# Queries and keys produced in natural layout, one graph at a time, with the values' product directly behind them

## The reference, cut to what matters

```python
x = x + gnn(layernorm(x), adj)          # 12 heads of 32
#   q, k, v = x@Wq.T, x@Wk.T, x@Wv.T + bv
#   a = softmax(q k^T * 384**-0.5 + adj) ; o = a v ; o@Wo.T + bo
x = x + ffn(layernorm(x))
#   top 2 of 4 experts by the graph's mean; h = act_e(u@w1_e.T + b1_e); y = sum gate * (h@w2_e + b2_e)
#   layernorm(y + u) * ln_g + ln_b      # u is the ffn's normalised input; act: gelu, silu, mish, gelu
```

## Time and profile before

| | before |
|---|---|
| three runs, us | 1636.82, 1639.47, 1640.29 (median 1639.47) |
| profiled execution, us | 1638.12 |
| its span, first to last instruction, us | 1636.0 |
| mean granted clock of the matrix engine | 0.993 of 2.4 GHz |
| stage 1, scores of step 3 to scores of step 63, us | 52.19 to 699.37 |
| length of a full step of stage 1, us | 10.70 |
| busy share of PE, DVE, ACT, POOL over the span | 97%, 74%, 58%, 42% |

### The profile page before, as it was taken

The page is one execution under the profiler, slowest core; times in us unless marked ns, Lnnn a source line. Parts: engine busy times, 40 slices in busy tenths (PEclk is TensorE's granted clock), DMA queues, the critical chain, the costliest instruction groups (busy, mean ns, idle before and its releaser), DMA issues.

```text
span 1636.0 us, 46011 instructions
## 1 busy us (share of the span) xinstructions
PE 1590.5 (97%) x12720; PEld 1528.0 (93%) x12721; DVE 1209.8 (74%) x3750; ACT 955.6 (58%) x2819; POOL 689.6 (42%) x1106
## 2 busy tenths in 40 slices
PE   8999999999999999779999999999999999999998
PEld 7999999999999999769999999999999999999998
DVE  5788888888888888657766666676776767677766
ACT  6899999999999988753422232333334323243332
POOL 3787888878888777531111111111111111111112
PEclk9999999999999999889999999999999999999999
DMA  6444433455545543673222222222222222222211
GB/s 190 153 138 138 136 129 132 147 168 182 176 169 172 182 134 133 253 301 105 71 74 74 74 74 74 74 74 74 67 70 71 65 74 74 74 74 65 83 59 45
DMA packets 93804, 189.09 MB, mean 116 GB/s; under 512 B 10337, under 2 KB 57441, under 8 KB 92385
## 3 DMA queue, kind: packets, MB, share of 16 engines
q1 hardware_dynamic: 91664, 170.17, 31.6%
q10 hardware_dynamic: 1872, 15.73, 2.5%
HBM read 108.80 MB, written 77.07 MB: 114 GB/s over the span
## 4 chain that ended last, share of the span: by engine, by line
PE 89%; DVE 3%; issue 2%; ACT 2%; DMA 1%; POOL 1%; DVEq 1%; ACTq 0%; POOLq 0%; SPq 0%
PE bank L460 69%; PE bank L534 5%; PE bank L667 5%; PE bank L487 3%; PE bank L557 3%; PE bank L574 2%; PE bank L543 1%; PE bank L566 1%; DMA ut_scratch<-ut_out 1%; DVE half_t L1371 1%; DVE inverse L1378 1%; DVE inverse L1374 1%; ACT at_hi L944 0%; ACT inverse L951 0%; ACT prob L737 0%
## 5 line engine op out<-in xcount | busy, mean ns | idle before, releaser
L460 PE MATMUL bank<-w_hi,ut_in 128*128 x1536 | 423.7, 343 | 0.8 <-issue 0.4
L460 PE MATMUL bank<-w_both,at_hi 128*128 x1524 | 389.1, 336 | 7.4 <-DVE at_lo L1343 7.3
L737 ACT ACTIVATE prob<-att,heads 128x128 f32<-128x128 f32 x768 | 297.4, 390 | 14.2 <-DVE heads L1108 10.3
L460 PEld LDWEIGHTS bank<-w_both,at_hi 128*128 128x128 f32 x1524 | 274.3, 188 | 12.3 <-issue 12.2
L460 PEld LDWEIGHTS bank<-w_hi,ut_in 128*128 128x128 f32 x1536 | 281.5, 189 | 1.3 <-issue 1.3
L460 PE MATMUL bank<-w_lo,ut_in 128*128 x768 | 258.2, 336 | 0.0
L460 PE MATMUL bank<-w_both,at_lo 128*128 x762 | 255.3, 335 | 0.0
L875 ACT ACTIVATE hid<-hid 128x384 f32<-128x384 f32 x192 | 95.1, 526 | 270.5 <-DVE hid L1264 270.5
L944 ACT ACTIVATE at_hi<-bank,gate_col 128x384 fp32r<-128x384 f32 x254 | 133.4, 576 | 199.6 <-PE bank L667 197.8
L1264 DVE TENSOR_TENSOR hid<-bank,b_wide 128x384 f32<-128x384 f32 x256 | 130.9, 552 | 147.6 <-PE bank L460 138.9
L1072 POOL TENSOR_SCALAR rs_z<-mv_z 128x1 f32<-128x1 f32 x64 | 34.9, 545 | 433.1 <-DVE mv_z L1397 433.1
(11 more groups left out here) (139 smaller groups left out, 3475.7 us busy)
## 6 DMA issues: line engine op xcount, KB each, us to landing
xu_scratch<-xu SPq DMA_DIRECT2D x64, 384.0 KB, 2.3
ut_scratch<-ut_out SPq DMA_DIRECT2D x64, 384.0 KB, 2.7
ut_in<-ut_scratch SPq DMA_DIRECT2D x64, 384.0 KB, 3.0
xz<-xu_scratch SPq DMA_DIRECT2D x64, 384.0 KB, 3.2
x_in<-in_x SPq DMA_DIRECT2D x32, 384.0 KB, 4.7
xu<-in_x SPq DMA_DIRECT2D x32, 384.0 KB, 4.3
out_dram<-xz SPq DMA_DIRECT2D x64, 192.0 KB, 2.2
w_lo<-in_L_ffn_w SPq DMA_DIRECT2D x4, 1152.0 KB, 5.9
```

Source lines behind the costliest of these rows:

```text
L460: last = nc.tensor.matmul(acc, lhs[c][a], rhs[c][b], start=start and n == 0, stop=stop and n == len(terms) - 1)
L737: nc.scalar.activation(prob[g][:, hh, :], att[g][:, head, :], ACT.Exp, bias=neg_max[g][:, head:head + 1], scale=-1.0, accum_out=row_sum[g] ...
```

## The change

Queries and keys of graph h+1 are made in step h, for one graph at a time and in natural layout: x's transposes are the stationary operand and the weights (384 columns) the moving one, 18 products. Both lie in one PSUM tensor `both` over banks 4 and 5. DVE copies them to memory (`take_qk` on DVE, 128x768), PE transposes them back into the same banks (`transpose_qk`, six transposes), and ACT copies these to `q_t` and `k_t`, of which there is now one set. The values of the same graph are made directly behind queries and keys and no longer between `spread_inverse` and `attend`. Everything that was made for graphs further ahead moves two steps nearer, the pipeline has two steps less ahead of the first scores, and x's transposes need half the memory.

u's transposes are stored unsplit (`take_u`), 192 KB instead of 384 KB for a graph. Stage 2 loads them and splits them there (`round_ut` on ACT, `rest_of_ut` on DVE), one graph ahead, behind the first job's activation.

The residual's x is loaded one step later but at the head of SP's step, and its output bias is added one step later (`add_output_bias(h - 2)`, ahead of the second norm's root on POOL). Memory is laid out anew: the first layers of three experts are loaded at steps 56, 57 and 58, the fourth at step 61, and the second layers in five transfers from step 63 on, the first of them (3.6 MB) over stage 1's projection weights.

The diff, cut to its core:

```diff
...
-        bank = [ps(f"bank{i}", [P, BANK]) for i in range(8)]
+        bank = [ps(f"bank{i}", [P, BANK]) for i in range(4)]
+        both = ps("both", [P, 2, BANK])
+        bank += [both[:, 0, :], both[:, 1, :]] + [ps(f"bank{i}", [P, BANK]) for i in range(6, 8)]
...
             def load_ut(b, m):
-                source = ut_dram[b] if isinstance(b, int) else ut_dram[bass.ds(b, 1)].rearrange("o p s c n -> (o p) s c n")
-                sp.dma_start(ut_in[m % 2][:].bitcast(F32), source).then_inc(ut_loaded[m % 2], 16)
+                source = ut_dram[b] if isinstance(b, int) else ut_dram[bass.ds(b, 1)].rearrange("o p c n -> (o p) c n")
+                sp.dma_start(ut_in[m % 2][:, 1].bitcast(F32), source).then_inc(ut_loaded[m % 2], 16)
...
+                if h % 2 == 1 and 2 <= t < PAIRS:
+                    for g in range(2):
+                        sp.wait_ge(xu_stored[t % 2][g], 16 * (t // 2))
+                    load_residual(t)
...
-                    reached(sp, ut_lo_done, n + 1)
-                    sp.dma_start(ut_dram[n], ut_out[n % 2][:].bitcast(F32)).then_inc(ut_stored[n % 2], 16)
-                if h % 2 == 0 and 2 <= t < PAIRS:
-                    for g in range(2):
-                        sp.wait_ge(xu_stored[t % 2][g], 16 * (t // 2))
-                    load_residual(t)
+                    reached(sp, ut_taken, n + 1)
+                    sp.dma_start(ut_dram[n], ut_out[n % 2][:]).then_inc(ut_stored[n % 2], 16)
...
-            def project_qk(h):
-
-                m, t = h % 2, pair(h + 2)
-                if h < 0:
-                    pe.wait_ge(wt_lo_done, (m + 1) * DC)
-                reached(pe, xt_lo_done, 2 * t + 2)
-                reached(pe, qk_done, qk_count(h - 1))
-                reached(pe, ot_done, h - 1)
-                reached(pe, inv_taken, h - 1)
-                for oc in range(DC):
-                    acc = bank[4 + oc // 2][:, (oc % 2) * 2 * N:(oc % 2 + 1) * 2 * N]
-                    last = split_product(acc, [(wt_hi[m][:, c, oc * P:(oc + 1) * P], wt_lo[m][:, c, oc * P:(oc + 1) * P]) for c in range(DC)],
-                                         [(xt_hi[t % 2][:, c, :], xt_lo[t % 2][:, c, :]) for c in range(DC)])
-                    if oc > 0:
-                        last.then_inc(qk_mm, 1)
+            def project_qk(n):
+
+                if n == 0:
+                    pe.wait_ge(wt_lo_done, 2 * DC)
+                reached(pe, xt_lo_done, n + 1)
+                reached(pe, ot_done, n - 2)
+                reached(pe, inv_taken, n - 2)
+                for m in range(2):
+                    last = split_product(both[:, m, 0:D], [(xt_hi[n % 2][:, c, :], xt_lo[n % 2][:, c, :]) for c in range(DC)],
+                                         [(wt_hi[m][:, c, :], wt_lo[m][:, c, :]) for c in range(DC)])
+                last.then_inc(qk_mm, 1)
+
+            def transpose_qk(n):
+                reached(pe, qk_taken, n + 1)
+                for m in range(2):
+                    for c in range(DC):
+                        last = nc.tensor.transpose(both[:, m, c * N:(c + 1) * N], qk_nat[:, m, c * P:(c + 1) * P], ident[:])
+                    last.then_inc(qkt_mm, 1)
...
 
                 reached(pe, inv_done, n + 1)
-                reached(pe, qk_done, qk_count(n + 1))
+                reached(pe, qk_done, 2 * min(n + 3, B))
                 reached(pe, inv_taken, n)
...
-                reached(pe, ut_loaded[m % 2], 16 * (2 * lap + m // 2 + 1))
+                reached(pe, ut_split, b + 1)
...
-                if has_qk(h):
-                    project_qk(h)
+                if has(h + 1):
+                    project_qk(h + 1)
+                    project_v(h + 1)
+                if h == -1:
+                    transpose_weights(3)
...
+                if has(h + 1):
+                    transpose_qk(h + 1)
...
-                if has(h + 2):
-                    project_v(h + 2)
...
-            def take_qk(h):
-                m, p = h % 2, slot(h + 2)
-                to, scale = (q_t[p], SCALE) if m == 0 else (k_t[p], 1.0)
-                reached(act, qk_mm, 2 * (h + 2) + 1)
-                nc.scalar.activation(to[:, 0:2, :], bank[4][:].rearrange("p (c n) -> p c n", c=2), ACT.Copy, scale=scale).then_inc(qk_done, 1)
-                reached(act, qk_mm, 2 * (h + 2) + 2)
-                nc.scalar.activation(to[:, 2, :], bank[5][:, 0:2 * N], ACT.Copy, scale=scale).then_inc(qk_done, 1)
+            def take_qk(n):
+                reached(act, s_mm, n)
+                for m, (to, scale) in enumerate(((q_t, SCALE), (k_t, 1.0))):
+                    reached(act, qkt_mm, 2 * n + m + 1)
+                    nc.scalar.activation(flat(to[:]), both[:, m, 0:D], ACT.Copy, scale=scale).then_inc(qk_done, 1)
 
             def take_probs(n, c):
                 reached(act, pt_mm, PTC * n + c + 1)
                 nc.scalar.activation(pt[c][:], bank[c][:], ACT.Copy).then_inc(pt_act, 1)
 
-            def round_u(n):
+            def take_u(n):
                 g = n % 2
                 reached(act, ut_mm, n + 1)
                 reached(act, ut_stored[g], 16 * (n // 2))
-                nc.scalar.activation(flat(ut_out[g][:, 0]), bank[3][:, 0:D], ACT.Copy).then_inc(ut_hi_done, 1)
+                nc.scalar.activation(flat(ut_out[g][:]), bank[3][:, 0:D], ACT.Copy).then_inc(ut_taken, 1)
...
+            def load_under_projections():
                 act.wait_ge(v_mm, B)
-                load_w1_hi(3)
-                load_w2("xt1", "xt1")
+                load_w2("unused", "wv")
...
+            def round_ut(b, m, lap):
+
+                reached(act, ut_loaded[m % 2], 16 * (2 * lap + m // 2 + 1))
+                nc.scalar.activation(flat(ut_in[m % 2][:, 0]), flat(ut_in[m % 2][:, 1]).bitcast(F32), ACT.Copy).then_inc(ut_rounded, 1)
...
-                if has_qk(h):
-                    take_qk(h)
-                    load_under_projections(h)
+                load_under_stages(h)
                 if has(h - 1):
                     take_probs(h - 1, 0)
                     take_probs(h - 1, 1)
+                if has(h + 1):
+                    take_qk(h + 1)
...
+                if has(h - 2):
+                    add_output_bias(h - 2)
...
-                if has(h - 1):
-                    add_output_bias(h - 1)
...
+            def take_qk(n):
+
+                reached(dve, qk_mm, n + 1)
+                reached(dve, qkt_mm, 2 * n)
+                nc.vector.tensor_copy(qk_nat[:], both[:, :, 0:D]).then_inc(qk_taken, 1)
...
-            def rest_of_u(n):
-                g = n % 2
-                reached(dve, ut_hi_done, n + 1)
-                nc.vector.tensor_tensor(flat(ut_out[g][:, 1]), bank[3][:, 0:D], flat(ut_out[g][:, 0]).bitcast(F32), ALU.subtract).then_inc(ut_lo_done, 1)
...
+            def rest_of_ut(b, m, lap):
+                reached(dve, ut_rounded, b + 1)
+                raw_half = flat(ut_in[m % 2][:, 1])
+                nc.vector.tensor_tensor(raw_half, raw_half.bitcast(F32), flat(ut_in[m % 2][:, 0]).bitcast(F32), ALU.subtract).then_inc(ut_split, 1)
...
+                if has(h + 1):
+                    take_qk(h + 1)
...
-                if has(h + 2):
-                    take_v(h + 2)
+                if has(h + 1):
+                    take_v(h + 1)
...
+                    if k == 0 and graph(b, 1) and not (isinstance(b, int) and b < 1):
+                        rest_of_ut(b + 1, (m + 1) % 4, lap + (m + 1) // 4)
...```

The end of a step's row on PE shows what now stands around `attend`. Before, from the transposes of the inverses (bank 5, L543; `inv_sum`) to the first of attend's products (bank 4, L557; `pt` are the transposed probabilities):

```order
L543 MATMUL bank5<-ident,inv_sum1 128x128 [waits inv_taken,qk_done,inv_done]
L543 MATMUL bank5<-ident,inv_sum1 128x128 x2
L460 MATMUL bank7<-wt_hi2,xt_hi0 128x384 [waits v_done,xt_lo_done]
L460 MATMUL bank7<-wt_lo2,xt_hi0 128x384
L460 MATMUL bank7<-wt_hi2,xt_lo0 128x384
L460 MATMUL bank7<-wt_hi2,xt_hi0 128x384
L460 MATMUL bank7<-wt_lo2,xt_hi0 128x384
L460 MATMUL bank7<-wt_hi2,xt_lo0 128x384
L460 MATMUL bank7<-wt_hi2,xt_hi0 128x384
L460 MATMUL bank7<-wt_lo2,xt_hi0 128x384
L460 MATMUL bank7<-wt_hi2,xt_lo0 128x384
L557 MATMUL bank4<-pt0,v_sb01 32x128 [waits qk_done,v_done,ot_done,pt_vec,pt_act]
```

More of the change, by code:

```diff
@@ L89, in gnn_moe_kernel @@
         stage_lo = [sb(f"stage_lo{p}", [P, D], F32R, s1) for p in range(3)]
+        raw = ExitStack()
+        w_raw = [sb(f"w_raw{m}", [P, DC, D], F32, raw) for m in range(4)]
+        raw.close()
+        sb("free", [P, 5376], F32, s1)
+        x_in = [sb(f"x_in{p}", [P, 2, D], F32, s1) for p in range(2)]
+        xt_hi = [sb(f"xt_hi{g}", [P, DC, N], F32R, s1) for g in range(2)]
+        xt_lo = [sb(f"xt_lo{g}", [P, DC, N], F32R, s1) for g in range(2)]
+        qk_nat = sb("qk_nat", [P, 2, D], F32, s1)
+        q_t = sb("q_t", [P, DC, N], F32, s1)
+        k_t = sb("k_t", [P, DC, N], F32, s1)
+        xn = [sb(f"xn{g}", [P, D], F32, s1) for g in range(2)]
```

(45 more changed lines are left out.)

155 lines of the change are left out of this document (62 added, 93 removed).

## The result

The changed kernel takes 1715.22 us (median of 4 runs, 1714.73 to 1717.36), the kernel before 1639.68 beside it (1636.82 to 1640.29): ratio 1.0467, 95% interval 1.0449 to 1.0485, 75.5 us more. The span of the profiled execution is 1713.2 us.

A forecast was written before the change was run, and what follows sets the result against it. Stage 1 was taken as bound by PE, busy all the time. 1638.1 + 71.6 + 1 + 2 + 4 = 1716.7 us for the profiled execution, with 1.4 to the median: 1718 us, range 1668 to 1742.

The forecast's parts named there:

- The step as laid out: Full step of stage 1, from scores to scores, with PE's waits: 12.04 us against 10.70 before.
- PE's own work: PE's work in a stage 1 step without waits: 11.06 us, 0.36 more than before, with 0.20 saved on the values.
- Six transposes: Transposing queries and keys back on PE in each stage 1 step adds 0.65 us, at 0.109 spacing each.
- Attend 1.43 behind bank 2's transposes: In stage 1, without values between, attend starts 1.43 us after bank 2's transposes began, waiting for DVE's copy.
- The steps together: From the scores of step 3 to those of step 63: 718.8 us against 647.2, so +71.6.
- The stall at step 62: PE's 8.55 us wait for POOL goes: the residual's load is issued earlier than needed and two first layers move away.
- Before step 3: Pipeline fill gains 3 us, the first three steps cost 4 more: +1 us, bounds -3 to +4.
- After step 63: More second-layer and bias traffic before the first second layer: +2 us, bounds -5 and +8.
- stage 2: DVE's added subtraction of 0.55 delays about half of 16 mish jobs: +4 us, bounds 0 and +9.
- PE's work alone: Rival: ACT and DVE answer sooner in stage 1, a step takes 11.1 to 11.5 us; chance 0.15.
- Not slower: Rival: the drain after stage 1 pays for all, near 1638 us; chance 0.04.
- Worse: Rival: stage 1 step of 12.4 or more through DVE's late division or a falling clock, 1745 to 1780 us; chance 0.13.

The follow-up runs named there:

- experiment 4: Changed kernel with ACT's normalisation of x moved early and the values' products put between bank 2's and the inverses' transposes: 1669.66 us, ratio 1.0175.
- experiment 1: Changed kernel with the values' products put back between the inverses' transposes and attend: 1688.47 us, ratio 1.0293.
- experiment 2: Changed kernel with the values' products moved behind the transposes of queries and keys: 1704.31 us, ratio 1.0392.
- experiment 5: Kernel before, old layout, with the values' products moved directly behind those of queries or keys: 1693.51 us, ratio 1.0328.
- experiment 3: Changed kernel with ACT's normalisation of x moved ahead of that of x1: 1706.03 us, ratio 1.0393.
- experiment 8: Changed kernel with the residual's load and the output bias put back at their old places on SP and POOL: 1719.78 us, ratio 1.0486.
- (9): Kernel before with the stage-2 loads of step 60 (first layers' biases, one first layer) issued later, in steps 63 and 61: 1631.11 us, ratio 0.9952.
- (11): Changed kernel with two more reductions of 128x384 per graph on DVE in stage 2, ahead of the added subtraction: 1725.19 us, ratio 1.0521.
- experiment 6: Kernel before with the residual's load a step later at the step's head and POOL's output bias one step later at its head: 1642.18 us, ratio 1.0014.

## Why the prediction came out

**The forecast, 1718, was 2.8 us high; in stage 1 its mechanism is the one that runs.** For the profiled execution it had 1716.7, which took 1715.47; the other 1.6 lie in the step to the median, which is 0.25 below that execution and not 1.4 above it. By its steps:

- *The step as laid out, 12.04:* 11.99, link by link. From the start of the scores, laid out and measured: bank 2's transposes 9.11 and 9.09, the inverses' 9.84 and 9.82, attend 10.54 and 10.52, x's 11.56 and 11.51. That is no luck of errors that cancel.
- *PE's own work, 11.06:* 11.22, so 0.16 too low. The layout's share is right, as experiment 4 shows (0.54 against 0.56). Wrong is the 0.20 that the values were to lose. Ahead of the values the inverses' transposes take 0.25 (412.70 to 412.95), ahead of attend 0.42 (experiment 4), so what the values' move saves is some 0.04. The step as laid out isn't touched by this, since it is added up block by block: without its waits it comes to 11.15 and not to 11.06.
- *Six transposes, 0.65:* 0.65 (410.21 to 410.86). Six times 0.27, the length of one, would be 1.6. The Trainium skill, "TensorE: Matmul & The Clock Gate", Part 4, gives about 275 ns for one transpose inside a kernel, behind a figure for bf16; these are float32, and this trace agrees with it as a length alone.
- *Keys late, 0.3:* 0.29 here, 0.30 in experiment 1.
- *Attend 1.43 behind bank 2's transposes:* 1.43, also in experiment 2 and, with the old layout, in experiment 5. That the missing values are the reason is shown from both sides: put back, the wait goes (1), taken away from the old layout, it comes (5).
- *x late, 0.23:* 0.20; experiment 3 removed it alone.
- *The steps together, +71.6:* +71.8. Of the 1.29 in each step, 0.87 comes with the new layout and the values in their old place (experiment 1; 0.54 of it work, 0.30 waiting for the keys), and 0.42 more with the values' new place.
- *The stall at step 62:* gone, so the term was right. The reason was given twofold, and only half of it holds: experiment 8 shows that it doesn't need the residual's new place. That loads out of the way end it is shown in the kernel before (9); for the kernel after it is argued only: there two first layers are loaded earlier (708.73 and 720.71) and the biases later (779.67), and the DMA share between 740 and 773 us is 0.16 to 0.41, where the kernel before has 0.97 and 1.00 from 670 to 690.
- *Before step 3, +1:* +2.0: the first three steps cost 4.1 more (predicted 4; not 1.3 each, but 2.1, 0.4 and 1.6), the fill gained 2.1 (predicted 3).
- *After step 63, +2, and stage 2, +4:* +0.1 up to the logits and +3.3 behind them. The traffic of second layers cost nothing, so that term was 2 too high. Stage 2's term came out in size but not for its reason: PE's waits for DVE grew by 0.9 there, and an estimated 1.8 is one fall of the clock, which the prediction didn't have. That the number came is luck. PE doesn't wait for the split of u, as predicted; with more work on DVE it does (11).

*PE's work alone* was wrong: an idle ACT didn't answer sooner, except where it was told to (3). *Not slower* was wrong: the drain paid for nothing but the stall. *Worse* was wrong in both mechanisms: the clock in stage 1 was 1.00 (54.21 to 773.17), and no step waited for DVE's division.

## What to carry to other kernels

An independent product is worth its place: here 1.6 us of values cover the turn-around of 1.43 from PE over DVE to PE and ACT's turn-around too (4), and where their inputs merely lie ready they cover nothing. Before a product is moved, measure the distance from what PE writes to where PE reads it back, and what stands between. And a step is early or late by its place in the queue, not by its number: a bias "one step later" that still stood ahead of ot_lo changed nothing (6), while loads of 2.7 MB that could be issued one and three steps later at no cost made a store late and cost 8 us (9).

## What was not expected

Two reductions of 0.54 per graph on DVE, 69 us over 64 graphs, cost 8.7 us in stage 2 (11), about half of it as waits of PE and most of the rest because the granted clock fell in two stretches more. So a wait of PE can cost more than its own length. When it does is open: in the kernel before and in experiment 6 PE waits the same 2.08 for DVE (at 768.52 and 770.75), and the clock behind it is 1.00 in the one (760 to 780) and 0.91 in the other (765 to 785).

And the change of kind ahead of and behind nine products isn't always 0.2: between transposes on both sides they took 1.67 (experiments 2 and 4), between transposes and attend 1.75 (408.84 to 410.59).
